# A decoder layer on one core: the order in which the shared expert's first two groups compute their units and their output products

## The reference, cut to what matters

```python
scores = sigmoid(xt @ w_router.T)            # 1024 tokens, 8 experts
topk_w, topk_i = top_k(scores, 2)
gate = silu(einsum('th,eih->tei', xt, wg)); up = einsum('th,eih->tei', xt, wu)     # inner width 640
expert_out = einsum('tei,ehi->teh', gate * up, wd)
out = einsum('te,teh->th', comb, expert_out)
sgate = silu(einsum('th,jih->tji', xt, sg)); sup = einsum('th,jih->tji', xt, su)   # 2 shared experts
out = out + einsum('tji,jhi->th', sgate * sup, sd)
x = layernorm(x + out)
```

## Time and profile before

| what | value |
|---|---|
| median of 3 runs | 770.0 us (769.99 to 773.52) |
| the profiled execution | 770.26 us, span 768.6 us |
| PE busy in the span | 706.3 us (92%) |
| DVE, ACT, POOL busy | 563.7, 472.8, 350.2 us |
| mean granted TensorE clock | 0.983 |
| 60 output products of group 0 | 9.65 us |
| 60 output products of group 1 | 7.20 us |
| a block's group, from one start to the next | 11.22 us |

### The profile page before, as it was taken

How to read it: one execution, slowest core, us unless ns; L and a number is a source line. 1 busy time by engine, 2 the same in 40 slices (tenths; PEclk the granted TensorE clock), 3 DMA queues, 4 the chain that set the end, 5 groups by cost and what they waited for, 6 DMA issues and landing times.

```text
span 768.6 us, 15115 instructions
## 1 busy us (share of the span) xinstructions
PE 706.3 (92%) x4958; PEld 640.7 (83%) x4958; DVE 563.7 (73%) x1174; ACT 472.8 (62%) x1066; POOL 350.2 (46%) x514
## 2 busy tenths in 40 slices
PE   4998888887999999999999996998999999999965
PEld 3888676676889999898999985877999999999855
DVE  4964688887878888888888885684778777776536
ACT  4444755447777777777777775353577776776401
POOL 0002566688998787878787775062000000000341
PEclk9999999999999999999999999899999999999978
DMA  9002400010200000000420030066376676660121
GB/s 296 4 1 81 174 1 1 1 34 28 63 8 2 7 0 7 0 7 0 140 71 0 0 104 1 3 245 215 117 234 197 229 252 198 223 220 29 56 68 56
DMA packets 45939, 64.81 MB, mean 84 GB/s; under 512 B 4288, under 2 KB 34880, under 8 KB 45632
## 3 DMA queue, kind: packets, MB, share of 16 engines
q1 hardware_dynamic: 40080, 56.45, 22.2%
q0 software_dynamic: 1536, 4.20, 1.7%
q10 hardware_dynamic: 4272, 3.51, 1.6%
HBM read 53.14 MB, written 11.01 MB: 83 GB/s over the span
## 4 chain that ended last, share of the span: by engine, by line
PE 61%; POOL 7%; DVE 4%; issue 4%; ACT 3%; another core or an unknown queue 1%; POOLq 0%; DVEq 0%; ACTq 0%
PE two L67 9%; PE two L69 7%; PE two L68 7%; PE bg L67 7%; PE bg L69 7%; PE bg L68 7%; PE bd L69 3%; PE bd L68 3%; PE bd L67 3%; PE two L321 3%; POOL under_dt L595 1%; PE two L296 1%; POOL under_raw L581 1%; POOL under_raw L576 1%
## 5 line engine op out<-in xcount | busy, mean ns | idle before, releaser
L1856 POOL DMA_INDIRECT gu_raw<-rows_out,slot x16 | 15.5, 971 | 201.3 <-DMA rows_out<-y_sb 196.7
L2002 ACT ACTIVATE sg<-bg 128x256 f32<-128x256 f32 (+1 forms) x95 | 40.7, 429 | 99.9 <-PE bg L69 89.5
L414 ACT ACTIVATE under_dt<-two,nb,under_raw 128x256 f32<-128x256 f32 x128 | 70.6, 562 | 44.8 <-DVE nb L497 44.8
L67 PE MATMUL bg<-xb_hi,gu_hi 128*128 128x256 f32 x300 | 86.2, 287 | 2.7 <-DVE xb_lo L2111 2.7
L69 PE MATMUL bg<-xb_hi,gu_lo 128*128 128x256 f32 x300 | 84.8, 283 | 0.0
L68 PE MATMUL bg<-xb_lo,gu_hi 128*128 128x256 f32 x300 | 84.8, 283 | 0.0
L2088 DVE TENSOR_TENSOR hf<-sg,bg 128x256 f32<-128x256 f32 (+1 forms) x95 | 45.0, 473 | 51.3 <-ACT sg L2002 49.2
L67 PE MATMUL two<-under_h 128*128 128x256 f32 (+1 forms) x208 | 66.9, 322 | 2.8 <-PEq L118 1.5
L68 PE MATMUL bd<-dn_lo,eh_hi 128*128 128x256 f32 x220 | 62.6, 285 | 3.4 <-issue 3.3
L69 PE MATMUL bd<-dn_hi,eh_lo 128*128 128x256 f32 x220 | 62.8, 286 | 2.1 <-issue 2.1
L595 POOL TENSOR_SCALAR under_dt<-under_dt,rec 128x256 f32<-128x256 f32 x128 | 62.3, 505 | 3.8 <-DVE rec L543 3.8
(11 more groups left out here) (292 smaller groups left out, 2532.9 us busy)
## 6 DMA issues: line engine op xcount, KB each, us to landing
gu_raw<-in_gu SPq DMA_DIRECT2D x17, 1280.0 KB
dn_raw<-in_dn SPq DMA_DIRECT2D x17, 640.0 KB
rows_in<-under_dt SPq DMA_DIRECT2D x1, 3840.0 KB, 13.1
rows_out<-y_sb SPq DMA_DIRECT2D x30, 128.0 KB, 2.1
x_blk<-rows_in ACTq DMA_DIRECT2D x13, 256.0 KB, 2.7
under_raw<-in_wq SPq DMA_DIRECT2D x1, 2048.0 KB, 8.0
under_raw<-in_wkv SPq DMA_DIRECT2D x1, 2048.0 KB, 12.6
under_raw<-in_wo SPq DMA_DIRECT2D x4, 512.0 KB, 4.0
```

What stands on the lines that cost most here:

```text
L67: pe.matmul(out, lh, rh, start=first, stop=False)
L414: act.activation(self.prob[:, g % 2, h, :], self.b_s[:, h // 2, (h % 2) * MW:(h % 2 + 1) * MW], ACT.Exp, bias=self.nb[:, h:h + 1], scale=s ...
L2002: act.activation(sg[:, u % 3, 0:width(u)], gate_of(u), ACT.Silu).then_inc(f_sg, 1)
```

## The change

Four edits, all in the order of the code:

- PE: group 1 runs its five units in a row. Then come `down(0)`, the first half of `down(1)` (two tiles), the turning of block 0, and the second half of `down(1)`. Group 2 has no `down` between its units any more; `down(2)` stays in group 3.
- ACT and DVE, group 1: `gate(7)` and `gated(7)` move ahead of unit 6's rounding; `round_dn(1)` and `rest_dn(1)` move behind unit 7's; unit 9's rounding moves from group 2's start to group 1's end.
- DVE: the eight `add` operations of groups 0 and 1 stood ahead of unit 7's and unit 12's work; all now stand at group 1's end, with block 0's `rest_x` ahead of the last two.
- `down` and `add` take a half as argument.

```diff
-            def down(q):
+            def down(q, part=None):
...
-                for t in range(4 if shared(q) else 2):
+                for t in range(4 if shared(q) else 2) if part is None else range(2 * part, 2 * part + 2):
...
                 gate_up(q, 0)
                 gate_up(q, 1)
-                if q:
+                if q >= 3:
                     down(q - 1)
-                else:
+                elif q == 0:
                     ranks()
...
                 gate_up(q, 4)
                 if q == 1:
+                    down(0)
+                    down(1, 0)
                     turn_block(0)
+                    down(1, 1)
...
@@ act_program
-                if q:
+                if q and q != 2:
                     round_h(IT * q - 1)
...
+                if q == 1:
+                    gate(IT * q + 2)
                 round_h(IT * q + 1)
...
                     round_gu(w, 1)
-                    round_dn(w)
-                gate(IT * q + 2)
+                    if q > 1:
+                        round_dn(w)
+                if q != 1:
+                    gate(IT * q + 2)
...
                 round_h(IT * q + 2)
+                if q == 1:
+                    round_dn(1)
                 gate(IT * q + 4)
                 round_h(IT * q + 3)
                 if q == 1:
+                    round_h(IT * q + 4)
                     round_x(0)
...
@@ dve_program
-                    rest_dn(w)
-                if q in (1, 2):
-                    add(q - 1)
+                    if q > 1:
+                        rest_dn(w)
...
                 if q == 1:
+                    rest_h(IT * q + 4)
+                    add(0, 0)
+                    add(0, 1)
+                    add(1, 0)
                     rest_x(0)
+                    add(1, 1)
```

More of the change, by code:

```diff
@@ L2113, in rest_x, with add @@
                                   ALU.subtract).then_inc(f_xlo, 1)
-            def add(q):
-                for t in range(4):
+            def add(q, half):
+                for t in range(2 * half, 2 * half + 2):
                     b = (q % 2) * 4 + t
@@ L2261, in dve_program @@
                     rest_gu(w, 0)
+                if q == 1:
+                    gated(IT * q + 2)
                 rest_h(IT * q + 1)
@@ L2287, in dve_program @@
                     norm(0)
+                if q == 1:
+                    rest_dn(1)
                 gated(IT * q + 4)
```

## The result

Before, 20 runs, with the three of the table above among them, had a median of 772.42 us, so the 770.0 that the prediction started from was one of the lower draws. The changed kernel's median of 20 was 776.25 (769.06 to 778.37). Without one slow run of 2384 us before, the ratio of the two is 1.0044, with a 95% interval of 1.0027 to 1.0061. A later comparison of the same kernel, 12 runs, gave 1.0026 (1.0007 to 1.0044). So the change costs 0.3 to 0.4%, some 2 to 3.4 us. That is within the 0.5% of "no change", but on the side opposite to the forecast, and 776.25 lies outside the forecast's range of 766.4 to 772.3. Even with the shift of the baseline taken out, 770.0 x 1.0044 = 773.4 is above its upper end.

What follows compares the result with a forecast made beforehand. PE's own work was taken to bound the kernel. The sum was 770.26 - 2.9 (earlier group 3) + 1.7 (clock) = 769.1 us, given as 769.0 for the median, with a range of 766.4 to 772.3.

Steps and rivals of the forecast that it cites:

- Part 5: Beside the scatter, PE's late signals could delay unit 9 and all behind it by 0 to 3.3 us; taken at 0.
- Part 1: PE's order in group 1: units 7 to 9 end at 519.6, the 2.47 us wait goes, group 2 starts at 534.4.
- the late cases: Signals of units 6, 7 and `down(0)` tiles beside the scatter, between 1.2 and over 4.4 us late before the change.
- Part 2: Group 2 without output products: its chain takes 10.74 us, PE stands 2.8 us, group 3 starts at 545.1, winning 2.9 us.
- Part 4: TensorE's clock could halve after group 2's new 2.8 us stand, costing 0 to 1.7 us; taken at 1.7.
- Part 3: Weights and rows: SP's order unchanged, group 4's load has over 10 us of cover; costed at nothing.
- The sign that the forecast had named: Forecast wrong if group 3 starts before 543.5 or after 547, or the tail from group 3 changes length.
- The rival of late signals: Unit 9 held waiting for unit 7's `hf`, deciding from a lag of 2.6 us; 770 to 772.4 us; chance 0.16.
- The 1.4: Us of signal lag that unit 7's `hf` was said to hide behind `gu_lo` before unit 9 is delayed.
- The forecast's last step: From the summed 769.1 us for the profiled execution to the median, shown 0.3 below it; given as 769.0.

Runs made afterwards that it cites:

- e3: Changed kernel with one of the scatter's sixteen indirect transfers, the other fifteen left out; group 3 started 43.04 us after the `slot` write.
- e6: Kernel before with one of the scatter's sixteen indirect transfers, the other fifteen left out; group 3 started 42.99 us after the `slot` write.
- e7: Changed kernel with 22 matmuls that nobody reads added after group 2's last unit to fill PE's stand; ratio to before 0.9997.
- e4: Changed kernel with the load of group 3's weights moved behind the scatter and the block rows; ratio to before 0.9961.
- e14: Second look at e4, the changed kernel with group 3's weights loaded behind the block rows; profiled execution 775.65 us.
- e5: Changed kernel with group 2's weights and group 3's `gu_raw` loaded ahead of the scatter, from expert 0; group 2 started 33.26 us after `slot`.
- e1: Changed kernel with `down(0)` put back between units 6 and 7; ratio to before 1.0131.
- e10: Changed kernel once more, no edit; group 3 started 46.27 us after the `slot` write.
- e8: Kernel before with the load of group 3's weights moved behind the scatter and the block rows; ratio to before 0.9977.
- e9: Kernel before once more, no edit; its 60 output products took 9.77 us, group 3 started 46.48 us after the `slot` write.

## Why the prediction was wrong

The step that failed is Part 5, the late signals, taken at 0 within bounds of 0 to 3.3 us. Counted from `slot`, against what the forecast gave:

| | forecast | after | after again |
|---|---|---|---|
| to unit 7 | 9.2 | 9.2 | |
| units 7 to 9 | 8.7 | 11.3 | |
| `down(0)` to group 2 | 14.8 | 15.8 | |
| group 2 starts at | 32.7 | 36.3 | 35.6 |
| group 2 to group 3 | 10.74 | 10.64 | 10.65 |
| group 3's first two units | 2.98 + 1.7 | 4.26 | 4.47 |

- **Part 1** failed with Part 5. PE's order and the work in it were right: e3 reproduces them to 0.3 us. But I let PE run at its own pace beside the scatter. Its signals were 2.6 to 5.6 us late, over the 1.4 us that unit 9 had in hand. Of the 3.6 us, 2.3 are waits of units 8 and 9 and 0.55 the wait for `acc`; the other 0.7 lie in small pieces.
- The reason I gave for 0 was that units 3 to 5 ran at 2.72 us beside the same scatter. That row shows a unit's pace on PE, and not when its signal reaches ACT. It also comes too early: in the changed kernel unit 5's signal was still in time (0.1 us), with a DMA share of 0.16 over the 3.8 us after `slot` and 0.63 over the unit itself. The lag began at unit 6, at a share of 0.93. The evidence on signals was in the late cases that I set aside because output products stood in front of them.
- **Part 2** was right: 10.64 us instead of 10.74, and a stand of 2.86 instead of 2.8. Yet its gain of 2.9 us was what `down(0)` lost beside the scatter (2.45) and unit 9's wait, and no part of it lay in group 2. e3 and e6 show this directly: with one transfer both orders start group 3 together. With all sixteen the new order paid the scatter's 3.4 us in another place, so nothing was left to win.
- **Part 4** was right in kind, and 0.2 to 0.4 us too high: the two units took 4.26 and 4.47, which is 1.3 and 1.5 over 2.98, and not 1.7. e7 shows that it is the stand. The same stand was followed by 4.47, 4.48 and 4.47 us in e3, e4 and e14 and by 5.29 us in e5, so 1.3 to 2.3 us in all.
- **Part 3** held: no wait for weights or rows before group 3.

The sign that the forecast had named was met too: group 3 started 46.93 us after `slot`, which is 548.6 in the time of the profile before, later than its 547. In sum, the stretch was to get 1.2 us shorter and got 1.6 longer. The 2.8 us between are 3.25 for group 2's start (mean of two profiles), less 0.1 for the chain and 0.3 for the clock. The rival of late signals named the right mechanism (unit 9's `hf`, deciding from 2.6 us of lag) and had 0.16. The lag is 4.0 us at the deciding unit, and the loss of 2.3 at units 8 and 9 lies close to the rule 4.0 - 1.4 = 2.6. The 1.4 was right by luck. The prediction took it from DVE's `gu_lo` ahead of unit 7's `hf`, but in e3 that `hf` came only 0.2 us behind its gate's end; 1.4 is what a unit's 2.72 us leave over the 1.3 us of ACT and DVE. The rival's 770 to 772.4 us were still too low. The runs before lie 2.4 us above the three shown, and with this taken out the ratio of 1.0044 gives 773.4, the later 1.0026 gives 772.0. The forecast's last step is also off by 0.2: 769.1 less 0.3 is 768.8, not 769.0.

Left open: how the scatter's transfers delay PE's signals inside the chip, and up to 1.8 us of the difference of the medians. The stages of these profiles hold 1.6 us of it. Since the ends of matmuls are modelled, the rows don't tell a late signal from work that itself ended later than modelled. That the scatter delays PE's supply of instructions is a rival for the "issue" stops inside the output products; no run tests it.

## What to carry to other kernels

Moving work out of a disturbed stretch wins only if what takes its place is not disturbed as well. Here the scatter cost 3.4 us whether output products or units stood beside it, and over 5 us more in e7, where unit 9 waited longer and ran at a clock of 0.50 after it. Before moving such a run out of a group, work out that group's chain through ACT and DVE without it: the products had covered 2.9 us of it, and the bare stand cost another 1.3 us of clock. Read a stand by what PE does next, and not by its label: where it ends with the tile that the unit waits for, it is that wait, though the profile says "issue". Take a term with bounds of 0 to 3.3 us from the row that shows the same quantity (when a signal arrives), not from a row that shows the engine's pace.

## What the runs showed of the hardware that was not expected

- Beside sixteen indirect transfers and the loads, 373 GB/s together, a unit's end reached ACT 2.6 to 5.6 us late, and 7.6 in e7. With one indirect transfer and 366 GB/s it arrived within 0.1 us, and with all sixteen but the loads moved away (89 to 102 GB/s) 1.9 us late.
- The same 60 products beside the same scatter took 9.65 and 9.77 us in one order and 14.68 and 15.77 in two others. In e1 PE stopped with "issue" as the reason; part of the time in both is a lower clock (0.85 and 0.71).
- A stand of 2.86 us in group 2 was followed by a clock of 0.65 over the next 4.26 us, while 2.64 us at unit 9 in e10 was followed by products at 1.00. In e3 the same stand gave 0.62 and in e5 0.50. A stand of 2.24 us in e8 was followed by 0.69, and one of 2.23 us before, in e6 and in e9 by 1.00. So in these rows the length of a stand alone doesn't say whether the clock falls.
